# Layer 1 of a graph network: the group mean and variance from sums made step by step, double buffers, and loops written out

## The reference

```
agg  = segment_sum(x[src], dst) / max(deg, 1)
f    = gelu(agg @ Wl.T + bl + x @ Wr.T)
mean = sum(f) / cnt
out  = f - mean_scale * mean
var  = sum(out * out) / cnt
out  = out / sqrt(var + EPS) * gn_weight + gn_bias
return out + x
```

## Time and profile before

| | |
|---|---|
| time, median of 3 runs | 2166.15 us (2165.77 to 2167.38) |
| time of the profiled execution | 2152.32 us |
| its span, first to last instruction | 2150.7 us |
| PE busy | 1959.9 us (91%) |
| DVE busy | 1510.5 us (70%) |
| ACT busy | 1234.0 us (57%) |
| stage of the change | 1657.3 to 1735.7 us of the span |

### The profile page before, as it was taken

The page is one execution under the profiler, slowest core; times in us unless marked ns, Lnnn a source line. Parts: engine busy times, 40 slices in busy tenths (PEclk is TensorE's granted clock), DMA queues, the critical chain, the costliest instruction groups (busy, mean ns, idle before and its releaser), DMA issues.

```text
span 2150.7 us, 62698 instructions
## 1 busy us (share of the span) xinstructions
PE 1959.9 (91%) x22393; PEld 1769.6 (82%) x22393; DVE 1510.5 (70%) x3127; ACT 1234.0 (57%) x3189; POOL 139.1 (6%) x120
## 2 busy tenths in 40 slices
PE   1149999999999999999999999999998878999997
PEld 1149999999999999999998777777888866888854
DVE  8588888888888888888886566666886366000066
ACT  5756666666666666666663788888896643000042
POOL 4700000000000000000000000000000053000001
PEclk7579999999999999999999999999999989999998
DMA  8412222222222222222223433333586169988722
GB/s 231 121 61 93 80 101 73 101 73 101 77 100 90 85 101 73 101 73 101 73 102 130 148 130 129 129 129 130 199 314 230 52 220 358 347 304 301 253 74 72
DMA packets 184484, 304.19 MB, mean 141 GB/s; under 512 B 12641, under 2 KB 135958, under 8 KB 184174
## 3 DMA queue, kind: packets, MB, share of 16 engines
q1 hardware_dynamic: 180506, 290.74, 38.6%
q0 software_dynamic: 3904, 12.50, 1.9%
HBM read 202.70 MB, written 100.48 MB: 141 GB/s over the span
## 4 chain that ended last, share of the span: by engine, by line
PE 81%; DVE 5%; ACT 5%; issue 3%; DMA 3%; POOL 1%; DVEq 1%; ACTq 0%; SPq 0%; POOLq 0%
PE ps L898 25%; PE ps L990 21%; PE ps L887 11%; PE ps L881 7%; PE ps L982 6%; PE ps L968 3%; PE ps L1179 2%; PE ps L1057 1%; POOL edge_area L724 1%; ACT edge_area L1315 1%; DMA hs<-node_rows 1%; PE ps L1065 1%; ACT edge_area L1268 1%; DMA edge_area<-x_stream 1%; DVE carry L1702 1%
## 5 line engine op out<-in xcount | busy, mean ns | idle before, releaser
L1315 ACT CAST edge_area<-ps 128x392 f16<-128x392 f32 x784 | 407.2, 519 | 393.4 <-PE ps L881 393.4
L898 PE MATMUL ps<-big,rows_area 128*128 128x128 f32 x4802 | 576.9, 277 | 0.0
L898 PEld LDWEIGHTS ps<-big,rows_area 128*128 128x128 f32 x4802 | 551.9, 192 | 0.0
L1321 ACT COPY big<-ps 128x392 f32<-128x392 f32 x784 | 416.9, 532 | 0.6 <-PE ps L887 0.3
L887 PE MATMUL ps<-edge_area 128*128 128x98 f16 x6272 | 416.2, 208 | 0.0
L1798 DVE TENSOR_TENSOR edge_area<-lo_pair,carry 128x1024 f16<-128x1024 f16 x392 | 268.6, 685 | 129.4 <-PE ps L887 125.9
L887 PEld LDWEIGHTS ps<-edge_area 128*128 128x128 f16 x6272 | 331.1, 97 | 0.0
L881 PE MATMUL ps<-edge_area 128*128 128x98 f16 x3136 | 276.0, 209 | 18.2 <-DVE edge_area L1804 11.7
L990 PE MATMUL ps<-big,agg 128*128 128x256 f16 (+1 forms) x2450 | 280.1, 272 | 0.0
L990 PEld LDWEIGHTS ps<-big,agg 128*128 128x128 f16 x2450 | 233.2, 98 | 25.9
L1799 DVE TENSOR_TENSOR edge_area<-cell_pair,carry 128x784 f16<-128x784 f16 x392 | 218.3, 557 | 0.0
(11 more groups left out here) (253 smaller groups left out, 1787.5 us busy)
## 6 DMA issues: line engine op xcount, KB each, us to landing
big<-edge_counts SPq DMA_DIRECT2D x315, 448.0 KB, 5.4
edge_counts<-edge_area SPq DMA_DIRECT2D x49, 1568.0 KB, 5.6
agg<-edge_counts SPq DMA_DIRECT2D x21, 448.0 KB, 6.6
hs<-node_rows POOLq DMA_DIRECT2D x14, 448.0 KB, 4.4
edge_area<-x_stream SPq DMA_DIRECT2D x14, 448.0 KB, 4.0
node_rows<-rows_area SPq DMA_DIRECT2D x1, 3136.0 KB, 13.3
agg_s<-node_rows SPq DMA_DIRECT2D x49, 64.0 KB, 4.9
agg_s<-in_x SPq DMA_DIRECT2D x49, 64.0 KB, 1.8
```

Of the source, the lines that this page charges most:

```text
L898: last = mm(p_sum, h0[:, n, :], w32[:, par, n, :], start=(n == 0), stop=(n == NB - 1))
L1315: nc.scalar.copy(store_slot[:, par, :, cols], p_count[s % 2]).then_inc(sem("count_taken"), 1)
L1321: nc.scalar.copy(w32[:, par, :, cols], p_weight[s % 4]).then_inc(sem("weight_taken"), 1)
```

## The change

The variance is no longer made from rows from which the mean of all steps has been subtracted. The first step's own mean (`centre`) is subtracted from each step as soon as its Gelu is there, so centring, squares and sums of both run in the same loop as the products. Afterwards some twelve small DVE operations make the true mean, the variance and the shift from the two sums (`mean0`, `off_mean`), and what is left of the mean goes into `shift`, which POOL adds.

The sum over a step's 7 blocks is now made on DVE (`over_step`, two reductions `"p b d -> p d b"` a step, which read with a step of 512 bytes), and PE sums only the result over the partitions, one product for each sum (`sum_rows`). Rows, their transposes and the aggregate have two buffers each (`h_pair`, `hT_pair`, `agg_pair`, PSUM `pA` and `pD`), the copy of the transposes goes from DVE to ACT, and all loops of the stage are written out. `pB` and `r_s` stay single.

```diff
+        hT_pair = (hT_s[:], big.view(NPAD, W))
+        agg_pair = (agg_s[:], big.view(NPAD + W, W))
+        h_pair = (hs[:], edge_area.view(2 * W, W).rearrange("p (b d) -> p b d", d=D))
+        moment = big.view(2 * NPAD - W, W).rearrange("p (n d) -> p n d", d=D)
+        block_sums = ((moment[:, 0, :], moment[:, 1, :]), (moment[:, 2, :], moment[:, 3, :]))
+        centre, mean0, off_mean = (moment[:, n, :] for n in (4, 5, 6))
...
-                sp.wait_ge(sem("sums_made"), 2)
+                sp.wait_ge(sem("sums_made"), 2 * NS + 1)
...
-            def load_rows(name, used):
-                pool.dma_start(hs[:], rows_of(rows_dram, 0)).then_inc(sem(name), 16)
-                with pool.Fori(0, NS - 1) as i:
-                    pool.wait_ge(sem(used), i + 1)
-                    pool.sem_inc(sem("passed"), 1)
-                    pool.dma_start(hs[:], rows_of(rows_dram, i + 1)).then_inc(sem(name), 16)
-                pool.wait_ge(sem(used), NS)
+            def load_rows():
+                for i in range(NS):
+                    if i > 1:
+                        pool.wait_ge(sem("hT"), i - 1)
+                    pool.dma_start(h_pair[i % 2], rows_of(rows_dram, i)).then_inc(sem(f"h_in2{'ab'[i % 2]}"), 16)
+                pool.wait_ge(sem("hT"), NS)
...
                 pool.drain()
+                pool.wait_ge(sem("gain_ready"), 3)
                 nc.gpsimd.tensor_tensor(norm, norm, over_rows(shift), ALU.add)
...
+            def rows_T(i):
+                pe.wait_ge(sem(f"h_in2{'ab'[i % 2]}"), i // 2 * 16 + 16)
+                if i > 1:
+                    pe.wait_ge(sem("hT_s"), i - 1)
+                transposes((pA, pD)[i % 2], h_pair[i % 2].rearrange("p b d -> p (b d)")).then_inc(sem("hT"), 1)
             def lin2(i):
                 pe.wait_ge(sem("agg_staged"), i + 1)
                 pe.wait_ge(sem("hT_s"), i + 1)
-                pe.wait_ge(sem("biased"), i + 1)
-                product(pB, [(agg_s, wt["WlT"][:]), (hT_s, wt["WrT"][:])]).then_inc(sem("lin2"), 1)
-            pe.sem_inc(sem("biased"), 1)
+                if i:
+                    pe.wait_ge(sem("biased"), i)
+                product(pB, [(agg_pair[i % 2], wt["WlT"][:]), (hT_pair[i % 2], wt["WrT"][:])]).then_inc(sem("lin2"), 1)
+            def sum_rows(i):
+                for n, rows in enumerate((f_all, sq_all)):
+                    sums = pC[:, n * TILE:n * TILE + D]
+                    pe.wait_ge(sem("rows_summed"), 2 * i + n + 2)
+                    last = mm(sums, ones[:], block_sums[i % 2][n], start=(i == 0), stop=False)
+                    if i == NS - 1:
+                        last = mm(sums, ones[0:LAST, :], rows[0:LAST, NB - 1, :], start=False, stop=True)
+                    last.then_inc(sem("sums_made"), 1)
             pe.wait_ge(sem("agg_done"), 2)
-            rows_T(2, "h_in2", 0)
-            def layer_1(i):
-                pe.wait_ge(sem("hT_s"), i + 1)
-                rows_T(2, "h_in2", i + 1)
+            rows_T(0)
+            rows_T(1)
+            lin2(0)
+            for i in range(1, NS):
+                if i + 1 < NS:
+                    rows_T(i + 1)
                 lin2(i)
-            mean_sums = summed(f_all, "gelu", "sums_made")
-            layer_1(0)
-            layer_1(1)
-            mean_sums(0, first=True)
-            with pe.Fori(2, NS - 1) as i:
-                layer_1(i)
-                mean_sums(i - 1)
-            lin2(NS - 1)
-            mean_sums(NS - 2)
-            mean_sums(NS - 1, last_step=True)
-            square_sums = summed(sq_all, "squared", "sums_made")
-            square_sums(0, first=True)
-            with pe.Fori(1, NS - 1) as i:
-                square_sums(i)
-            square_sums(NS - 1, last_step=True)
+                if i == 1:
+                    pe.wait_ge(sem("rows_summed"), 1)
+                    mm(pC[:, 0:D], ones[:], block_sums[1][0], start=True, stop=True).then_inc(sem("sums_made"), 1)
+                else:
+                    sum_rows(i - 2)
+            pe.wait_ge(sem("hT_s"), NS)
...
+            def stage_agg(i):
+                if i > 1:
+                    act.wait_ge(sem("lin2"), i - 1)
+                nc.scalar.copy(agg_pair[i % 2], sum1[:, i * W:(i + 1) * W]).then_inc(sem("agg_staged"), 1)
+            def copy_rows(i):
+                act.wait_ge(sem("hT"), i + 1)
+                nc.scalar.copy(hT_pair[i % 2], (pA, pD)[i % 2][:, 0:W]).then_inc(sem("hT_s"), 1)
             def gelu(i):
-                act.wait_ge(sem("biased"), i + 2)
-                nc.scalar.activation(f_all[:, bass.ds(i * SB, SB), :], blocks(r_s), ACT.Gelu).then_inc(sem("gelu"), 1)
+                act.wait_ge(sem("biased"), i + 1)
+                nc.scalar.activation(f_all[:, i * SB:(i + 1) * SB, :], blocks(r_s), ACT.Gelu).then_inc(sem("gelu"), 1)
+            def square(i):
+                act.wait_ge(sem("centred"), i + 1)
+                nc.scalar.activation(sq_all[:, i * SB:(i + 1) * SB, :], f_all[:, i * SB:(i + 1) * SB, :],
+                                     ACT.Square).then_inc(sem("squared"), 1)
             act.wait_ge(sem("agg_done"), 2)
             stage_agg(0)
-            with act.Fori(0, NS - 1) as i:
-                act.wait_ge(sem("lin2"), i + 1)
-                stage_agg(i + 1)
+            copy_rows(0)
+            stage_agg(1)
+            copy_rows(1)
+            for i in range(NS):
+                if i + 2 < NS:
+                    stage_agg(i + 2)
+                    copy_rows(i + 2)
                 gelu(i)
-            gelu(NS - 1)
-            with act.Fori(0, NS) as i:
-                act.wait_ge(sem("centred"), i + 1)
-                nc.scalar.activation(sq_all[:, bass.ds(i * SB, SB), :], f_all[:, bass.ds(i * SB, SB), :],
-                                     ACT.Square).then_inc(sem("squared"), 1)
+                if i > 0:
+                    square(i - 1)
+            square(NS - 1)
...
-            def copy_rows(i):
-                dve.wait_ge(sem("hT"), i + 1)
-                V.tensor_copy(hT_s[:], pA[:, 0:W]).then_inc(sem("hT_s"), 1)
-            copy_rows(0)
-            dve.wait_ge(sem("lin2"), 1)
-            copy_rows(1)
-            add_bias(0, True)
-            with dve.Fori(1, NS - 1) as i:
-                dve.wait_ge(sem("lin2"), i + 1)
-                copy_rows(i + 1)
-                add_bias(i)
-            add_bias(NS - 1)
-            dve.wait_ge(sem("sums_made"), 1)
-            V.scalar_tensor_tensor(out=scaled_mean[:], in0=pC[:, 0:D], scalar=1.0 / N_NODES, in1=bcast["mean_scale"][:],
-                                   op0=ALU.mult, op1=ALU.mult)
-            dve.drain()
-            with dve.Fori(0, NS) as i:
-                f = f_all[:, bass.ds(i * SB, SB), :]
-                V.tensor_tensor(f, f, over_blocks(scaled_mean), ALU.subtract).then_inc(sem("centred"), 1)
+            def step_of(t, i):
+                return t[:, i * SB:(i + 1) * SB, :]
+            def over_step(out, rows, count):
+                return V.tensor_reduce(out, rows[:, 0:count, :].rearrange("p b d -> p d b"), AX_X, ALU.add).then_inc(
+                    sem("rows_summed"), 1)
+            def centred(i):
+                dve.wait_ge(sem("gelu"), i + 1)
+                f = step_of(f_all, i)
+                V.tensor_tensor(f, f, over_blocks(centre), ALU.subtract).then_inc(sem("centred"), 1)
+            def sum_steps(i):
+                whole = SB if i < NS - 1 else SB - 1
+                if i > 1:
+                    dve.wait_ge(sem("sums_made"), 2 * i - 1)
+                dve.wait_ge(sem("centred"), i + 1)
+                over_step(block_sums[i % 2][0], step_of(f_all, i), whole)
+                dve.wait_ge(sem("squared"), i + 1)
+                over_step(block_sums[i % 2][1], step_of(sq_all, i), whole)
+            add_bias(0)
             V.tensor_tensor(shift[:], bcast["gn_bias"][:], bcast["bc"][:], ALU.add)
             V.tensor_tensor(last_share[:], out_cnt[:, 1, :], inv_cnt[:], ALU.mult)
+            dve.wait_ge(sem("gelu"), 1)
+            over_step(block_sums[1][0], step_of(f_all, 0), SB)
+            add_bias(1)
+            dve.wait_ge(sem("sums_made"), 1)
+            V.tensor_scalar(centre, pC[:, 0:D], 1.0 / W, None, ALU.mult)
+            dve.drain()
+            centred(0)
+            for i in range(2, NS):
+                add_bias(i)
+                centred(i - 1)
+                sum_steps(i - 2)
+            centred(NS - 1)
+            sum_steps(NS - 2)
             dve.wait_ge(sem("fold_made"), 1)
             V.tensor_copy(clique_out[:], pA[:, 0:D])
-            V.tensor_scalar(gain[:], pC[:, 0:D], 1.0 / N_NODES, EPS, ALU.mult, ALU.add).then_inc(sem("gain_ready"), 1)
-            dve.wait_ge(sem("std_ready"), 1)
-            V.reciprocal(scaled_mean[:], gain[:])
-            dve.drain()
-            V.tensor_tensor(gain[:], scaled_mean[:], bcast["gn_weight"][:], ALU.mult)
-            dve.drain()
-            dve.sem_inc(sem("gain_ready"), 1)
+            dve.drain()
```

(66 more changed lines are left out.)

## The result

The changed kernel took 2183.2 us (median of 4 runs, 2180.97 to 2184.52), the kernel before 2165.96 beside it (4 runs): ratio 1.0078, 95% interval 1.0066 to 1.0089. The change makes the kernel slower by 17 us. Predicted were 2183, with 2163 to 2192 as the range.

The account below looks back on a forecast made before the run. The prediction took a closed ring of waits between TensorE and DVE to bound the loop. Terms -6.3, +14.6 and -3.7 make +4.6 us warm; with +12 for the clock, about +17 on 2166.15 gives 2183, range 2163 to 2192.

Parts of the forecast that it names:

- Where the kernel is bound: Layer-1 loop: TensorE's small sums wait for DVE's reductions, next transposes and products wait behind them, and DVE waits for those.
- Fill, -6.3: Stage start until lin2(0) is done: second row buffer lets both transposes run at once, 1662.9 in place of 1669.19.
- R = 1.8: Time in us of one DVE reduction of 896 f32 read 512 bytes apart, chosen at 1.95 ns each.
- The rival of the contiguous price: Stepped DVE reductions cost only 1.09 us, as contiguous ones, while TensorE's clock falls: about +5 us, 2171; chance 22%.
- Ring 6.5 + 2R: One warm loop step, DVE and TensorE waiting in turn: 6.5 us plus two reductions, 10.0 against 5.9.
- Loop 50.0 warm: From lin2(0) to lin2(6) with TensorE at full clock: 50.0 us in place of 35.4, +14.6.
- Tail -3.7 (27.4 us): From lin2(6) to DVE's add of the normalised rows: 27.4 us against 31.1, square sums gone but reductions added.
- the fold: Folding of the weights before lin3(0), near the stage's end: 2 us more, with the wait there, from TensorE's lower clock.
- Clock, +12: TensorE's clock falls in idle times: 2.1 us in each of five loop steps, 10.5, and 2 more before lin3(0).
- the faster one: Whole stage: reductions at contiguous price and TensorE's clock holds, together -5.8 us, 2160; chance 12%.

Follow-up runs that it names:

- the second profile: Profile of the changed kernel run again as it is, against the kernel before, in a later session: 2166.47 us, ratio 1.0077.
- the version with 24 products: Changed kernel plus 24 extra identity products a step on TensorE, after lin2(i) and ahead of the sums: 2158.57 us, ratio to the kernel before 1.0037.
- the control: The changed kernel run again, nothing edited, beside the kernel before in a later session: 2166.47 us against 2150.38, ratio 1.0077.

## Why the prediction was right

- *Where the kernel is bound*: right. TensorE waits for `rows_summed` with the next transposes and products behind it, and DVE waits for those. Moving the sums by one step (2141.5) shows that this wait is the cause, and nothing else in the loop.
- *Fill, -6.3*: right. 5.5 us against 11.75.
- *R = 1.8*: a little high, 1.66 (0.15 off on some 15 reductions, 2 us in all), but reached by a wrong reading, and so partly luck. The 1.57 ns of the 12-byte row are 401 ns over 256 elements, with the fixed part left in, while the contiguous rows had their 154 ns taken off. Read alike, the row has 0.96 ns an element ((401 - 154) / 256), and a contiguous reduction of 256 would take 420 ns. So beside a reduction that row isn't "already half dearer", and like the row of 13 elements it spoke for R = 1.09. It doesn't bear out the rule of the Trainium skill (Advanced Engine Details and Errata, Memory Cachelines) either, as the prediction has it. The choice of twice the contiguous price had only that rule and the 2-byte write of L1702 on its side, and neither gave a size; the measured 1.70 ns an element is the first row with a longer step. The rival of the contiguous price is refuted by 1.08 against 1.66.
- *Ring 6.5 + 2R*: 9.8 to 9.9 by the measured R (1.66, and 1.70 in that version), 9.80 measured with the clock held. With R = 1.08 it gives 8.66, and 8.55 was measured.
- *Loop 50.0 warm*: 50.3. Two errors cancel: R, and a DMA wait that I had said wouldn't be there. The rows of step 2 are issued at 1674.9, when the transposes of step 0 are done, and land 5.62 us later, 1.5 us after TensorE wants them (1.0 in the second profile). Behind them on the chain come ACT's copy and its table load, then the first Gelu:

```profile
1674.90 5.62 DMA hs<-node_rows
...
1680.56 1.00 PE ps L1053 x7
...
1682.50 1.28 ACT L1434
```

  Two buffers don't help the third load.
- *Tail -3.7 (27.4 us)*: 28.6 in both profiles, and 2 of it is the clock of the fold, which I had put under the clock: 26.6 against 27.4, the rest again R.
- *Clock, +12*: the mechanism is right, the size 2 too high. In the loop 8.2 us, not 10.5: the price of a step is as put (1.6 to 2.7, mean 2.1, by the adds of the second profile and of the version with 24 products), but four steps pay it, not five. `lin2(2)` comes before the first long idle time (add to add 4.6 us in both versions). The fold costs 2.0, as put: from the square root to the end mark it is 12.7 us against 10.7 before, and TensorE's clock is 0.50 from 1753 to 1763, where before it was 1.00 until 1728.
- The sum of the terms was 16.6, the stage's loss 14.2 to 14.6. The time's was 17.2 in the session of the result and 16.0 in the control. So the 2183.0 is nearer than the terms deserve: 1.5 to 3 us of the difference don't lie in the stage by the profiles, and stay open.
- *Of the rivals*, the faster one (contiguous price and warm clock, 5.8 under before) was put at one place with R as its price. Made on purpose, it gave a stage 1.8 us shorter than before, with the fold's clock (2 us) not held; 0.9996 in time. The one with the contiguous price and a falling clock, "about +5", gave +3.8 in the stage and +6.6 in time; its sum had left out the 2 us of the fold.

## What to carry to other kernels

Before a new operation is put into an in-order queue, write down what it waits for and what stands behind it: a product of 0.1 us that waited for two reductions of its own step cost 25 us, and the same product one step later none. A gain in one half of a change (here 9 us by double buffers, a moved copy and written-out loops together) can hide that the other half loses more, so time the halves apart. Work that moves from a busy engine to another should move back where the first is idle: in the loop DVE had the time for the reductions, in the tail TensorE had it. And when a price per element is taken from a row, take the fixed part off every row or off none.

## What the runs showed of the hardware

- A DVE reduction over seven f32 words 512 bytes apart took 1.66 us for 896 elements, over neighbouring words 1.08, in the same kernel. An element cost 1.70 ns stepped and 0.98 contiguous. The read with a step of 12 bytes in the earlier trace rows, another kind of operation, took 401 ns for 256 elements, no more than the 420 of a contiguous reduction of that size, which is an estimate from the same rows.
- TensorE's clock fell in each step of the loop with an idle time of 3.75 us, one small product and another 0.8 to 1.1 us, and again with 3.2 and 0.5 us in the version with contiguous reads; it held through idle times of 0.6 us. Extra products that nobody needs, and that end just before the awaited operand is there, gave back 8.2 us of the loop; 1.5 us too long, they gave back 2.0.
- The stepped reductions took 1.67 to 1.76 us in the loops of the versions with late sums or extra products, where TensorE was busier, and 1.65 to 1.68 in the changed kernel. The contiguous ones took 1.08 us with extra products and without. What makes the difference isn't shown.
- A small DVE operation (L2228 in the changed kernel, 128x128) took 2.21 us in place of 0.29 in all nine profiles that have it, each time as it started together with POOL's multiplication of a whole step (L789, 2.07 us). From the timeline after:

```profile
1755.49 2.21 DVE L2228 TENSOR_TENSOR shift<-shift,scaled_mean 128x128 f32<-128x128 f32 x1
1755.49 2.07 POOL L789 TENSOR_TENSOR big<-big,gain 128x896 f32<-128x896 f32 x1 [32.21 <-DVE gain L2224]
1758.38 2.07 POOL L792 TENSOR_TENSOR big<-big,shift 128x896 f32<-128x896 f32 x1 [0.83 <-DVE shift L2228]
```

It didn't delay POOL, whose gap of 0.8 us stood there before as well.
- The same code ahead of the stage took 14 to 17 us more in the profiled execution of the result than in the eleven others, the first of the kernel before among them, with DVE waiting 0.5 to 1.2 us ahead of single small instructions and once 8.3 us between 60 and 80 us of the span. What causes it was not found. Compare stages within a profile, and times only beside the kernel before in the same session.
